# First stage: values mixed for two query tiles at a time, and tokens normalized in place in their turned layout

## The reference, cut to what matters

```
x = x + attention(layernorm(x), ctx, ctx)      # 16 heads of 32, biases on q, k, v and output
x = x + experts(layernorm(x))                  # 32 experts x 4 sets, one token of each 32 to an expert
x = x + mlstm(layernorm(x), ctx, ctx)          # 8 heads of 64, gated
x = x + bitlinear_ffn(layernorm(x))            # ternary weights, 8-bit activations
```

## Time and profile before

| | |
|---|---|
| median of 3 runs | 2037.43 us (2035.82 to 2038.3) |
| the profiled execution | 2041.76 us, its span 2040.0 us |
| first phase | from 0 to about 1080 us |
| PE busy | 1795.0 us, 88% of the span |
| DVE busy | 1256.1 us, 62% |
| ACT busy | 1262.1 us, 62% |
| POOL busy | 604.0 us, 30% |

### The profile page before, as it was taken

One profiled execution on the slowest core, in us unless ns is written; L12 is line 12 of the kernel. 1 busy time (PEld: TensorE's weight loads), 2 busy tenths in 40 slices (PEclk: granted clock), 3 DMA queues, 4 the chain that ended last, 5 costly groups with the idle time before them and its releaser, 6 DMA issues. The chain is left out here.

```text
span 2040.0 us, 40464 instructions
## 1 busy us (share of the span) xinstructions
PE 1795.0 (88%) x14768; PEld 1091.9 (54%) x14818; DVE 1256.1 (62%) x2571; ACT 1262.1 (62%) x2479; POOL 604.0 (30%) x1108
## 2 busy tenths in 40 slices
PE   6999999999999999999985876636699999999877
PEld 2666666666666666666652543215365455555543
DVE  1766757758577686776663564423566766766662
ACT  1675666666666666666661554312587887887865
POOL 1343123321233232322300000004545545535630
PEclk9999999999999999999996998757699999999989
DMA  7453435534346354443422658978436436435200
GB/s 237 117 136 99 148 102 148 141 90 147 111 118 180 92 171 125 103 141 95 118 84 93 196 166 353 414 278 279 126 109 203 141 115 223 135 109 168 79 21 21
DMA packets 167315, 302.44 MB, mean 148 GB/s; under 512 B 26128, under 2 KB 74320, under 8 KB 158928
## 3 DMA queue, kind: packets, MB, share of 16 engines
q1 hardware_dynamic: 126352, 213.43, 32.9%
q10 hardware_dynamic: 24384, 52.84, 7.7%
q0 software_dynamic: 16384, 33.59, 7.0%
HBM read 165.31 MB, written 67.34 MB: 114 GB/s over the span
## 5 line engine op out<-in xcount | busy, mean ns | idle before, releaser
L572 DVE TENSOR_REDUCE a_negmax<-a_score 128x1 f32<-128x512 f32 x512 | 346.3, 683 | 112.8 <-PE a_score L711 105.3
L453 ACT ACTIVATE a_prob<-a_score,a_negmax 128x512 f32<-128x512 f32 x512 | 353.7, 693 | 97.5 <-DVE a_negmax L572 97.1
L334 POOL DMA_DIRECT2D a_q_stack<-a_q_parts x512 | 251.1, 499 | 533.8 <-DVE a_q_parts L566 261.4
L711 PE MATMUL a_score<-a_k_stack,a_q_stack 128*128 128x512 f32 x512 | 357.7, 699 | 20.7 <-ACT a_prob L453 12.6
L719 PEld LDWEIGHTS a_turn<-a_ident,a_prob 128*128 128x128 f32 x2048 | 253.9, 141 | 137.1 <-issue 95.7
L719 PE MATMUL a_turn<-a_ident,a_prob 128*128 128x128 f32 x2048 | 309.3, 274 | 3.6 <-ACT a_perm L429 1.9
L342 ACT COPY a_probT<-a_turn 128x512 f32<-128x512 f32 x256 | 149.9, 586 | 250.0 <-PE a_turn L719 249.0
L342 DVE COPY a_probT<-a_turn 128x512 f32<-128x512 f32 x256 | 176.1, 688 | 202.2 <-PE a_turn L719 202.0
L711 PEld LDWEIGHTS a_score<-a_k_stack,a_q_stack 128*128 128x128 f32 x512 | 97.6, 191 | 137.5 <-issue 81.1
L2078 PE MATMUL c_ff<-c_w1T,c_xqT 128*128 128x512 bf16 x489 | 131.9, 391 | 22.2 <-ACT c_xqT L1637 10.5
L793 PE MATMUL a_work<-a_cT,a_Wk 128*128 128x512 f32 x256 | 133.6, 617 | 10.7 <-DMA a_Wk<-in_L_xattn_Wk 10.7
(11 more groups left out here) (223 smaller groups left out, 3065.5 us busy)
## 6 DMA issues: line engine op xcount, KB each, us to landing
a_k_stack<-a_k_parts SPq DMA_DIRECT2D x512, 64.0 KB, 2.8
a_q_stack<-a_q_parts POOLq DMA_DIRECT2D x512, 64.0 KB, 2.5
scratch_res<-b_chosen SPq DMA_DIRECT2D x32, 1024.0 KB, 11.0
c_res<-scratch_res SPq DMA_DIRECT2D x32, 1024.0 KB, 8.8
a_weights<-in_ffn_W ACTq DMA_DIRECT2D x16, 1024.0 KB, 4.9
c_negm<-scratch_m SPq DMA_DIRECT2D x64, 256.0 KB, 4.6
a_xs<-in_x ACTq DMA_DIRECT2D x8, 1024.0 KB, 6.0
a_x<-in_x ACTq DMA_DIRECT2D x8, 1024.0 KB, 5.9
```

The lines of the kernel that those rows point to most:

```text
L334: eng.dma_start(stack[kind][i * DH0:(i + 1) * DH0, M % 2, g, :].bitcast(F32), parts[kind][g * DH0:(g + 1) * DH0, part, :].bitcast(F32)).th ...
L453: nc.scalar.activation(prob[:, U % 4, :], score.bank(U)[:, :], ACT.Exp, bias=negmax[:, u:u + 1], accum_out=sums[:, head_of(U), tile_of(U): ...
L572: nc.vector.tensor_reduce(negmax[:, U % UNITS:U % UNITS + 1], score.bank(U)[:, :], AX.X, ALU.max, negate=True).then_inc(max_ready, 1)
L711: nc.tensor.matmul(score.bank(U)[:, :], stack["Q"][:, M % 2, g, t * P:(t + 1) * P], stack["K"][:, M % 2, g, :], start=True, stop=True).the ...
```

## The change

**Mixing.** The mixing of two query tiles is done in one step instead of two: every eighth step (u = 2, 10, 18, 26, 34, 42, 50, 58) `mix_values` runs twice, for the tile due then and for the one that was due four steps earlier. The turned probabilities, kept in 8 slots before, get 10 slots, numbered by unit.

**Tokens.** For the first batch nothing changes, but that its normalized tokens lie in the slots of the turned probabilities. For the other seven: the turns XT, their copies by ScalarE, and VectorE's `tile_result` of u = 21 to 24 are gone. In place of them

- VectorE copies mean and inverse deviation of the 512 tokens into 8 columns (u = 21),
- TensorE turns these into 8 rows (NM, u = 23), ScalarE copies them and stores them in DRAM (4 KB, u = 24), and loads them, spread over all 128 partitions, as `norm_rows` (512 KB, u = 26),
- ScalarE's queue loads the next batch's tokens already turned (a host layout `x_T`) into `xT` (1 MB, u = 28, once the last product that reads `xT` is done),
- VectorE waits at u = 33 for both and subtracts the means (u = 33 to 36) and multiplies by the inverse deviations (u = 37 to 40), one pass of 128x512 in each step, both inputs in SBUF, in place,
- the Q product at u = 44 waits for these passes instead of the copies.

The tokens `xs` are still loaded, for the statistics.

```diff
@@ -211,6 +211,8 @@
     AHEAD = 2
     MIX_AT = HM + 2
 
+    SLOTS = 2 * HM + 2
+
     QUERY_PARTS, KEY_PARTS = (0, 0, 1, 1), (0, 1, 0, 1)
 
 
@@ -225,12 +227,11 @@
                 (40, 1, "K", 0, 1), (44, 1, "Q", 0, 1), (48, 2, "L", 0, -1), (50, 1, "V", 1, 1), (54, 1, "V", 2, 1),
                 (58, 1, "V", 3, 1), (62, 2, "K", 1, 1))
 
-    TURNS = ((1, "R", 3, -1), (17, "R", 0, 0), (33, "R", 1, 0), (35, "XT", 0, 1), (37, "XT", 1, 1), (39, "XT", 2, 1), (41, "XT", 3, 1),
-             (43, "NT", 0, -1), (45, "NT", 1, -1), (46, "NT", 2, -1), (47, "NT", 3, -1), (49, "R", 2, 0), (54, "PM", 0, -1),
+    TURNS = ((1, "R", 3, -1), (17, "R", 0, 0), (23, "NM", 0, 1), (33, "R", 1, 0), (43, "NT", 0, -1), (45, "NT", 1, -1), (46, "NT", 2, -1), (47, "NT", 3, -1), (49, "R", 2, 0), (54, "PM", 0, -1),
              (58, "SUM", 0, 0))
     FIRST_TURNS = [("XT", 0, c) for c in range(C)]
     FIRST_PRODUCTS = [("K", 0, 0), ("V", 0, 0), ("V", 0, 1), ("Q", 0, 0), ("V", 0, 2), ("V", 0, 3), ("K", 0, 1)]
-    STATS_AT, SCALE_AT, RESULT_AT = 13, 17, 21
+    STATS_AT, SCALE_AT, COLUMNS_AT, ROWS_AT, ROWS_IN, RESULT_AT = 13, 17, 21, 26, 28, 33
     CHOICE_AT, PERM_AT = 51, 57
 
     PIECE_UNITS, PIECE_AT, PIECE_STEP = ALL // (2 * PIECES), 8, 4
@@ -339,7 +346,7 @@
             def probs_out(copy, eng, U):
 
                 turn.wait_full(eng, 0, entries["P", U])
-                copy(probT[:, U // HM % 2, U % HM, :, :],
+                copy(probT[:, U % SLOTS, :, :],
                      turn.bank(entries["P", U])[:, :].rearrange("p (k q) -> p k q", k=T)).then_inc(turn.free[entries["P", U] % 2], 1)
 
@@ -414,6 +421,13 @@
                     j = entries[kind, b, n]
                     turn.wait_full(act, 0, j)
                     src = turn.bank(j)[:, :]
+                    if kind == "NM":
+                        if b > 1:
+                            act.wait_ge(norm_stored, (b - 1) * 16)
+                        nc.scalar.copy(norm_turned[:, :], turn.bank(j)[0:2 * T, 0:P]).then_inc(turn.free[j % 2], 1)
+                        turn.wait_read(act, 0, j)
+                        act.dma_start(scratch["norm"][b], norm_turned[:, :]).then_inc(norm_stored, 16)
+                        return
                     if kind == "R":
                         if b or n:
                             mix.wait_read(act, 0, b * GROUPS + n - 1)
@@ -452,6 +466,14 @@
                     u = U % UNITS
                     nc.scalar.activation(prob[:, U % 4, :], score.bank(U)[:, :], ACT.Exp, bias=negmax[:, u:u + 1],
                                          accum_out=sums[:, head_of(U), tile_of(U):tile_of(U) + 1]).then_inc(score.free[U % 3], 1)
+
+                def load_norm(b):
+                    act.wait_ge(norm_stored, b * 16)
+                    if b > 1:
+                        act.wait_ge(xT_ready, b - 1)
+                    act.sem_inc(act_parted, 1)
+                    act.dma_start(norm_rows[:, :, :].rearrange("p k s -> p (k s)"),
+                                  scratch["norm"][b].rearrange("k p -> (k p)").partition_broadcast(P)).then_inc(norm_in, 16)
 
                 def load_weights(w):
 
@@ -532,6 +554,11 @@
                             round_weights(piece, k)
                         if rest == 3 and piece >= PIECES:
                             store_weights(piece, k)
+                    if u == ROWS_AT and b + 1 < B:
+                        load_norm(b + 1)
+                    if u == ROWS_IN and b + 1 < B:
+                        work.wait_full(act, 0, jobs["Q", b, GROUPS - 1])
+                        act.dma_start(xT[:, :, :], A["x_T"][b + 1]).then_inc(xT_in, 16)
                     if r == PIECE_OUT and piece < 2 * PIECES:
                         if piece == PIECES:
                             act.dma_start(scratch["wscale"], wscale[:, :]).then_inc(wscale_stored, 16)
@@ -565,6 +592,13 @@
                     dve.wait_ge(hi_ready, b * (2 * GROUPS) + (2 * n + (kind == "Q") + 1))
                     nc.vector.scalar_tensor_tensor(parts[kind][:, 1, :], work.bank(j)[:, :], {"K": bk, "Q": bq}[kind][:, n:n + 1],
                                                    parts[kind][:, 0, :].bitcast(F32), ALU.add, ALU.subtract).then_inc(work.free[j % 2], 1)
+
+                def norm_columns(b):
+                    if b > 1:
+                        turn.wait_full(dve, 0, entries["NM", b - 1, 0])
+                    nc.vector.tensor_copy(norm_cols[:, 0, :], norm0.mv[:, :, 0])
+                    chain.step(nc.vector.tensor_copy(norm_cols[:, 1, :], norm0.rstd[:, :]))
+                    dve.sem_inc(norm_ready, 1)
 
                 def maximum(U):
 
@@ -666,14 +700,21 @@
                             last = norm0.tile_stats(xs, u - STATS_AT)
                         if u == STATS_AT + T - 1:
                             norm0.moments(dve, chain, last)
+                            dve.sem_inc(xs_read, 1)
                         if SCALE_AT <= u < SCALE_AT + 4:
                             norm0.scale(chain, (u - SCALE_AT,))
-                        if RESULT_AT <= u < RESULT_AT + T:
-                            last = norm0.tile_result(xs, xn, u - RESULT_AT)
-                        if u == RESULT_AT + T - 1:
+                        if u == COLUMNS_AT:
+                            norm_columns(b + 1)
+                        if u == RESULT_AT:
+                            dve.wait_ge(xT_in, (b + 1) * 16)
+                            dve.wait_ge(norm_in, (b + 1) * 16)
+                        if RESULT_AT <= u < RESULT_AT + 2 * C:
+                            k, c = divmod(u - RESULT_AT, C)
+                            last = nc.vector.tensor_tensor(xT[:, c, :], xT[:, c, :], norm_rows[:, k, :], (ALU.subtract, ALU.mult)[k])
+                        if u == RESULT_AT + C - 1:
                             chain.step(last)
-                            dve.sem_inc(xn_ready, 1)
-                            dve.sem_inc(xs_read, 1)
+                        if u == RESULT_AT + 2 * C - 1:
+                            last.then_inc(xT_ready, 1)
                     if b >= 1:
                         if u in (37, 38):
                             norm1.scale(chain, (2 * (u - 37), 2 * (u - 37) + 1))
@@ -738,7 +779,7 @@
                         for g in range(HM):
                             h = M % GROUPS * HM + g
                             last = nc.tensor.matmul(mix.bank(M)[g * DH0:(g + 1) * DH0, cols], v[:, b % 2, k, h * DH0:(h + 1) * DH0],
-                                                    probT[:, q % 2, g, k, :], start=k == 0, stop=k == T - 1, skip_group_check=True)
+                                                    probT[:, (q * HM + g) % SLOTS, k, :], start=k == 0, stop=k == T - 1, skip_group_check=True)
                     if t == T - 1:
                         last.then_inc(mix.full[0], 1)
 
@@ -752,8 +793,14 @@
                         nc.tensor.matmul(turn.bank(j)[:, 0:2], one[:, :].to_broadcast([P, P]), w_sum[:, :],
                                          start=True, stop=True).then_inc(turn.full[j % 2], 1)
                         return
+                    if kind == "NM":
+                        turn.wait_free(pe, 0, j)
+                        pe.wait_ge(norm_ready, b)
+                        nc.tensor.transpose(turn.bank(j)[0:2 * T, 0:P], norm_cols[:, :, :].rearrange("p k t -> p (k t)"),
+                                            ident[:, :]).then_inc(turn.full[j % 2], 1)
+                        return
@@ -773,10 +820,13 @@
                     j = jobs[kind, b, n]
                     cols = slice(n * P, (n + 1) * P)
                     if 0 in steps:
-                        turned = {("Q", 0): "XT", ("L", 0): "NT"}.get((kind, n))
+                        turned = "NT" if kind == "L" else "XT" if kind == "Q" and n == 0 and b == 0 else None
                         if turned:
                             for c in (C - 2, C - 1):
                                 turn.wait_read(pe, 0, entries[turned, b, c])
+                            pe.sem_inc(pe_parted, 1)
+                        if kind == "Q" and n == 0 and b > 0:
+                            pe.wait_ge(xT_ready, b)
                             pe.sem_inc(pe_parted, 1)
@@ -817,7 +867,8 @@
                     if 1 <= g <= ALL:
                         turn_probs(g - 1)
                     q, rest = divmod(g - MIX_AT, HM)
-                    if rest == 0 and 0 <= q < ALL // HM:
+                    if rest == 0 and q % 2 == 1 and 0 <= q < ALL // HM:
+                        mix_values(q - 1)
                         mix_values(q)
```

More of the change, by code:

```diff
@@ L272, in attention_phase @@
         x1 = sb("x1", [P, T, D])
-        xn, xn1 = sb("xn", [P, T, D]), sb("xn1", [P, T, D])
+        xn1 = sb("xn1", [P, T, D])
+        norm_cols, norm_turned, norm_rows = sb("norm_cols", [P, 2, T]), sb("norm_turned", [2 * T, P]), sb("norm_rows", [P, 2, S])
         xT, cT = sb("xT", [P, C, S]), sb("cT", [P, 2, C, S])
@@ L278, in attention_phase @@
         prob = sb("prob", [P, 4, S])
```

(14 more changed lines are left out.)

## The result

The changed kernel takes **2064.85 us** (median of 4 runs, 2061.1 to 2067.03) beside 2037.87 for the kernel before on the same chip (4 runs): ratio **1.0129, 95% interval 1.0109 to 1.015**. It is slower, by more than the predicted range allowed (2024 to 2048). The profiled execution took 2061.1 us, its span 2059.3.

What follows compares the result with a forecast made beforehand. TensorE was taken to bound the first stage. Batches 1 to 6 gave +1.2 us, batch 0 -1.8, batch 7 -1.0 and its last steps +2: +0.4 in all, given as 2037.5 us on the median's footing, range 2024 to 2048.

Steps and rivals of the forecast that it cites:

- Smaller terms: Steps 23 and 8 lose 0.3 us a batch each; the added transfers cost nothing, landing 2.4 us before needed.
- rival D: Turned tokens land in xT after VectorE asks, 1 to 2 us a batch: +10 us, 2047; chance 0.06.
- Pairs: Two mixes in one step take 2.08 us against 2.40, saving 0.33 a pair, 8 pairs a batch.
- rival E: A pair of mixes saves only one set of edges, 0.14 us less each: +6 us, 2043; chance 0.11.
- Turns: TensorE's four token turns, 0.44 us each, leave each of 7 batches: 1.76 us a batch saved.
- the small turn: One added TensorE turn of 8 columns per batch, between 0.1 and 0.6 us, taken as 0.3.
- The rule for VectorE: A score starts at least 1.56 us after VectorE ends three steps earlier; steps 36 to 43 stall 3.7 us more a batch.
- rival B: VectorE catches up: the stall of steps 36 to 43 grows only 1.5 to 2 us a batch; 2025; chance 0.25.
- The sum without transfers: All terms with transfers at nothing: +0.2 us in each of batches 1 to 6, batch 0 -1.8, total +0.4.
- Rival C, the clock: Idle TensorE in late steps 39 to 42 lowers its clock, 2 to 3 us in six batches: +15, 2052; chance 0.12.
- K stack's wait in step 8: ScalarE's wait for the K stack's transfers is fixed in time, so the pair at 2 saves nothing: +0.3 us a batch.

Runs made afterwards that it cites:

- e6: e1 without the eight normalizing passes, so Q of batches 1 to 7 comes from unnormalized tokens: 2028.17 us, 0.9939 of the kernel before.
- e2: The kernel before with mixing in pairs alone, tokens normalized in place in xs and xs loaded at u = 44: 2034.45 us, 0.997 of the kernel before.
- e1: The changed kernel with the loads of xs and cT issued at u = 46 instead of 26: 2039.25 us, 0.9997 of the kernel before.

## Why the prediction was wrong

**The step that failed** is the one in "Smaller terms": "I cost them at nothing, with a cover of 2.4 us". Its working took the loads' rate of the earlier trace rows for the 3.5 MB that the change puts between steps 26 and 33 and had them in after 13.3 us. Measured in batch 3: 20.6 us (490.58 to 511.17). The rate was about right (2.1 MB in 7.6 us are 276 GB/s, and 291 were measured). The bytes were not: 6.16 MB and not 3.67 passed, because the load of weights two steps ahead and the K and Q stacks of the next group, which begin at step 30, use the same 16 DMA engines. No run took the weights or the stacks away, so their part is arithmetic: the 2.5 MB more are 8.6 us at 291 GB/s, and the landing was 7.3 later than the 13.3 worked out. In the kernel before both are in the trace; the earlier trace rows showed two loads issued 3 us after the weights' load and landed two us after the first of the stack's transfers was issued, so for the most part in the gap between them. The time of VectorE's question was right: 15.7 us after step 26's loads predicted, 15.8 measured. So rival D was the truth, with 0.06 and a price of 10 us. Its mechanism was named and its size was off by a factor of three: its waits were 32.2 us in six batches, 5.4 each, not 1 to 2 a batch.

**The rest, point by point.**
- *Pairs*: 1.88 us from first matmul to the next product (1.9 forecast), 3.61 a step (forecast 3.61). Right; rival E falls.
- *Turns*: gone; the small turn takes 0.27. Right.
- *The rule for VectorE*: the scores of 39 to 43 forecast at 6.96, 9.35, 12.33, 14.1 and 17.4 after that of 36. Batch 6 above: 6.94, 9.33, 12.31, 14.17, 17.49. Right to 0.1 us, and rival B falls, since the stall has the forecast size. Its cause was split wrong, though: without the passes (e6) the steps still take 15.5 where nothing hindered would be 12.8, so the passes make 1.9 of the 3.7 that the stall grows by. The rest was there without them. Pairs alone (e2) lengthen 36 to 43 from 15.0 to 15.9, though a pair should save 0.33: that is 1.2 for the mix that left step 38 for 42. What is left, about 0.6, goes with the three turns that filled waits of these steps before; no run shows that part alone.
- *The sum without transfers*: +0.4 us forecast; e1, which is the change with its transfer landed in time, 0.9997 in the whole and -2.5 at the last score. Per batch +0.2 forecast for 1 to 6; +0.03 measured (779.2 us in e1, 779.0 before). Batch 0 gained 4.0, not 1.8, and the last one lost 2.5, not 1. These two errors partly cancel, so that the total came out as close as it did is in part luck.
- *Rival C, the clock*: it did come, but seldom from the late steps alone. In e1, where xT is in time, steps 38 to 42 of batch 3 and those of four more of the six batches ran at a granted clock of 1.00, that is 2.4 GHz. In batch 1 of e1 it fell all the same, behind a wait of step 39 for VectorE's maximum:

```profile
238.38 0.59 PE L752 MATMUL a_score<-a_k_stack,a_q_stack 128*128 128x512 f32 x1 [2.14 <-ACT a_prob L467]
```

```profile
236.00:240.00 4.00, 1.86 (x7) 1.46 (x7) 3.66 (x11) 0.83 (x3) 0.00 (x0) 0.83 0.71 264
240.00:244.00 4.00, 3.61 (x10) 1.54 (x9) 3.79 (x11) 2.28 (x6) 0.00 (x0) 0.74 0.02 4
```

There 36 to 43 took 17.8 us instead of 17.4: 0.4 in one batch, not 2 to 3 in each of six. In the changed kernel the clock fell in each of batches 0 to 4, in part to its other level of 1.2 GHz, as in the 0.72 and 0.66 at 376 and 645 us behind waits for xT, with TensorE busy 8.25 of 12 us and 6.39 of 10. How much of the 27.8 us this makes was not separated from the waits. An upper estimate: in the stretches of 5 us below full clock (0.85, 0.81, 0.66, 0.79, 0.53, 0.94, 0.72, 0.76, 0.56) what is missing to full speed adds up to 12 us. The Trainium skill (TensorE: Matmul & The Clock Gate, A second HAM failure mode) tells of short, frequent idles between groups of matmuls that make the clock swing. The traces agree with it in part: the late steps of e1 have such idles in all six batches (up to 1.78 us in batch 3), and the clock fell in one of them; in the changed kernel three of the five falls came behind one longer wait instead, of a score held up by the wait for xT (5.7, 5.1 and 4.1 us in batches 0, 2 and 4).
- *K stack's wait in step 8*: the +0.3 is not shown for the change. Step 9 took 2.42 us in the mean of batches 1 to 7 of the changed kernel and 2.12 before, but 2.05 in e1, and in these three kernels it lies anywhere from 1.5 to 3.1 from batch to batch. With pairs alone (e2) it is 2.57.

## What to carry to other kernels

A load's landing time read from a trace holds for the traffic it met there; before a transfer is put on a queue, list all that every queue carries from its issue to its deadline, and count the bytes against the rate. When work is moved off a busy engine, its price on the receiving engine is set by the step that it goes to: the same eight passes cost 12 us or at most 2. And a store that the same engine waits for should not share a queue with large loads: any rearrangement of the loads can then become a wait.

## What the runs showed of the hardware

- 64 KB transfers of the K stack needed 2.9 us to landing in batch 3 before the change and 7.2 beside the large loads of another queue after it. Queues of different engines did not shield each other: their shares of DMA time added up to 99.5%.
- The 1 MB load of xT took 5.5 us to landing (median) with neither of the two loads of step 26 ahead on its queue, 9.3 to 9.8 with one and 14.0 with both.
- Per byte the stacks' transfers were dearer than the large loads: the SyncE and GpSimd queues moved 1.41 of 6.16 MB (23%) in the stretch shown for 30.4% of the engines' time. No run tells whether that comes from the size of their packets.
- Executions of the kernel before on one chip spread from 2032 to 2046 us. The cause was not looked for.
